# Attention plus recurrence on one core: another order of TensorE's work in the attention slots

## The reference

```python
def attn(x, Wq, Wkv_short, Wkv_long, Wo, mix_weight, decay_factor):   # x: 16 x 512 x 256, 16 heads of 16
    decay_bias = -jnp.abs(pos[None, :] - pos[:, None]) * (1.0 - decay_factor)
    out_short = _attention(q, k_s, v_s, decay_bias)      # softmax(q k^T / 4 + bias) v
    out_long = _attention(q, k_l, v_l, None)
    out = alpha * out_short + (1.0 - alpha) * out_long
    return out @ Wo                                        # heads side by side again
...
x = _layernorm(x + attn(x, ...))
x = _layernorm(x + ffn(x, ...))    # gated recurrence over the 16 sequences, then tanh
```

## Time and profile before

| | |
|---|---|
| median of 3 runs | 2291.74 us (2289.07 to 2291.78) |
| the profiled execution | 2290.99 us |
| its span, first to last instruction | 2289.2 us |
| TensorE busy over the span | 2101.6 us, 92% |
| VectorE busy | 1663.5 us, 73% |
| ScalarE busy | 1476.8 us, 65% |

### The profile page before, as it was taken

One profiled execution on the slowest core, in us unless ns is written; L12 is line 12 of the kernel. 1 busy time (PEld: TensorE's weight loads), 2 busy tenths in 40 slices (PEclk: granted clock), 3 DMA queues, 4 the chain that ended last, 5 costly groups with the idle time before them and its releaser, 6 DMA issues.

```text
span 2289.2 us, 42658 instructions
## 1 busy us (share of the span) xinstructions
PE 2101.6 (92%) x16472; PEld 1126.9 (49%) x16472; DVE 1663.5 (73%) x2106; ACT 1476.8 (65%) x1758; POOL 174.1 (8%) x203
## 2 busy tenths in 40 slices
PE   2999999999999999999999999999999869999950
PEld 1444444444444444444444444444444348888840
DVE  2788888888888888888888788888888723333367
ACT  1477777777777777777777777676767643333336
POOL 0000000000000000000000000000000000000038
PEclk8799999999999999999999999999999979999975
DMA  2222222222222222222222222222222130000017
GB/s 77 47 64 55 53 63 54 62 61 57 63 54 62 54 62 55 62 54 63 55 62 54 62 55 62 64 52 63 53 53 54 36 113 28 27 27 27 18 37 220
DMA packets 127657, 134.27 MB, mean 59 GB/s; under 512 B 39778, under 2 KB 85602, under 8 KB 127474
## 3 DMA queue, kind: packets, MB, share of 16 engines
q1 hardware_dynamic: 98306, 98.74, 18.3%
q10 hardware_dynamic: 29168, 33.03, 4.7%
HBM read 37.77 MB, written 16.78 MB: 24 GB/s over the span
## 4 chain that ended last, share of the span: by engine, by line
PE 86%; ACT 5%; SPq 2%; POOL 2%; issue 2%; DVE 1%; DMA 0%; ACTq 0%; POOLq 0%; DVEq 0%
PE pv_ps L615 22%; PE pair_ps L551 17%; PE work L525 14%; PE pair_ps L577 11%; PE gate_ps L1050 11%; PE work L677 4%; PE pair_ps L533 3%; PE work L1043 2%; ACT probs L327 2%; SPq L199 2%; ACT pv_sb L382 2%; POOL rstd L806 1%; POOL veps L804 1%; PE work L681 1%; PE work L1034 1%
## 5 line engine op out<-in xcount | busy, mean ns | idle before, releaser
L493 DVE TENSOR_REDUCE maxes<-pair_ps 128x2 f32<-128x1024 f32 x1024 | 1247.4, 1223 | 277.4 <-PE pair_ps L533 171.6
L327 ACT ACTIVATE probs<-pair_ps,small 128x1024 f32<-128x1024 f32 x512 | 570.0, 1114 | 250.1 <-PE pair_ps L533 242.8
L327 ACT ACTIVATE probs<-pair_ps 128x1024 f32<-128x1024 f32 x512 | 523.1, 1023 | 180.1 <-PE pair_ps L551 175.8
L615 PE MATMUL pv_ps<-probs,vals 128*32 128x512 f32 x4096 | 547.5, 607 | 0.6 <-ACT probs L327 0.5
L551 PE MATMUL pair_ps<-q_op,k_op 56*128 56x512 f32 (+1 forms) x2048 | 512.4, 498 | 3.6 <-DMA q_op<-shift_rows 2.8
L577 PE MATMUL pair_ps<-k_op,q_op 55*128 55x512 f32 x2048 | 439.4, 425 | 29.3 <-DMA q_op<-kq_l 18.4
L551 PEld LDWEIGHTS pair_ps<-q_op,k_op 56*128 56x128 f32 (+1 forms) x2048 | 191.3, 184 | 554.8 <-issue 525.2
L577 PEld LDWEIGHTS pair_ps<-k_op,q_op 55*128 55x128 f32 x2048 | 196.3, 187 | 94.4 <-ACT probs L327 34.5
L533 PE MATMUL pair_ps<-eye_b,tri_b 64*128 64x64 bf16 x4096 | 152.3, 194 | 0.0
L292 POOL TENSOR_TENSOR o_sum<-o_att 128x512 f32<-128x512 f32 x32 | 40.9, 1278 | 1306.7 <-DVE o_att L460 1306.7
L533 PEld LDWEIGHTS pair_ps<-eye_b,tri_b 64*128 64x128 bf16 x4096 | 90.4, 96 | 92.3 <-issue 72.1
(11 more groups left out here) (129 smaller groups left out, 2467.9 us busy)
## 6 DMA issues: line engine op xcount, KB each, us to landing
k_op<-kq_h SPq DMA_DIRECT2D x1024, 32.0 KB, 2.0
k_op<-kq_l SPq DMA_DIRECT2D x512, 32.0 KB, 2.0
q_op<-kq_h SPq DMA_DIRECT2D x512, 32.0 KB, 2.0
x_step<-in_xT ACTq DMA_DIRECT2D x16, 512.0 KB, 4.1
q_op<-kq_l SPq DMA_DIRECT2D x256, 32.0 KB, 2.0
x_res<-in_x ACTq DMA_DIRECT2D x16, 512.0 KB, 4.6
x_dram<-res ACTq DMA_DIRECT2D x16, 512.0 KB, 3.4
x_back<-x_dram SPq DMA_DIRECT2D x16, 512.0 KB, 4.8
```

The costliest lines, as they stand in the source:

```text
L327: act.activation(probs[:, s % 2, 2 * hp:2 * hp + 2, :], pairs_ps[pair_of(b, s, 2 * hp)][:, :, :], ACT.Exp, scale=LAM if s // 4 % 2 else 1. ...
L493: dve.reduce_max(maxes[:, u % 2, :, hp, s % 4], pairs_ps[pair_of(b, s, 2 * hp + 1)][:, :, :], mybir.AxisListType.X).then_inc(a_reduced, 1)
L615: last = pe.matmul(pv_ps[32 * h:32 * h + 32, :], vals[:, c, g // 2, att, at:at + 32], probs[:, s % 2, h, :], start=(c == 0), stop=(c == TC ...
```

## The change

TensorE's work is written in bodies of two slots. With `s` even, the order is: task of `s`; a stretch of three pairs; `weigh` of slot `s-2`; a stretch of two pairs; `weigh` of slot `s-1`; a stretch of three pairs; task of `s+1`. So the task of an odd slot stands next to the task of the even slot behind it. `weigh` now runs two slots behind (`LAG`), and `probs` has three buffers for two (`PROBS`). In each slot the pair for the maxima now comes ahead of the pair for the weights. The tasks are laid out anew: slots 0 and 28 have none, two slots (23 and 27) do both halves of a `kq`, all `turn` tasks stay at slots 1, 5, ..., 29. On ScalarE the part of the task now comes ahead of both exponentials, and the copy of `pv_ps` moves to slots 1, 5, ..., 29. On VectorE the part of the task stands between the two maxima in odd slots and ahead of both in even slots. The number of matmuls, exponentials and maxima is the same.

```diff
-TASKS = {0: ("ot", 0, -1), 2: ("v", (4,), 0), 3: ("v", (5,), 0), 4: ("v", (6,), 0), 6: ("ot", 1, -1), 7: ("v", (7,), 0),
...
+TASKS = {2: ("v", (4, 5), 0), 3: ("ot", 0, -1), 4: ("v", (6,), 0), 6: ("v", (7,), 0), 7: ("ot", 1, -1), 8: ("wo", (0,), -1),
+         12: ("wo", (1,), -1), 16: ("wo", (2, 3), -1), 20: ("v", (0,), 1), 22: ("v", (1,), 1), 24: ("v", (2,), 1), 26: ("v", (3,), 1),
+         10: ("kq", (1, (0,)), 1), 11: ("kq", (1, (1,)), 1), 14: ("kq", (0, (0,)), 1), 15: ("kq", (0, (1,)), 1),
+         18: ("kq", (2, (0,)), 1), 19: ("kq", (2, (1,)), 1), 23: ("kq", (4, (0, 1)), 1), 27: ("kq", (3, (0, 1)), 1),
+         30: ("kq", (5, (0,)), 1), 31: ("kq", (5, (1,)), 1)}
...
+LAG, PROBS = 2, 3
...
# ScalarE
+                    if s % 4 == 1:
...
+                            act.activation(pv_sb[:, u % 2, :], pv_ps[:, :], ACT.Copy).then_inc(pv_copied, 1)
+                    part_or_values(b, s)
                     if exists(b):
                         exp_pair(b, s, 0)
-                    part_or_values(b, s)
-                    if exists(b):
                         exp_pair(b, s, 1)
...
# VectorE
-                    reduce(0)
+                    if s % 2:
+                        reduce(0)
                     if has_task(b, s):
...
+                    if s % 2 == 0:
+                        reduce(0)
                     reduce(1)
...
# TensorE
             def body(b):
-                for s in range(SLOTS):
-                    scores(b, s, 0)
-                    if has_task(b, s):
-                        work_task(b, s)
-                    scores(b, s, 1)
-                    bb, ss = (b, s - 1) if s else (b - 1, SLOTS - 1)
-                    if exists(bb):
-                        weigh(bb, ss)
+
+                for s in range(0, SLOTS, 2):
+                    work_task(b, s)
+                    scores_for_max(b, s, 0)
+                    scores(b, s, 0)
+                    bias_for_max(b, s, 0)
+                    bias(b, s, 0)
+                    scores_for_max(b, s, 1)
+                    bias_for_max(b, s, 1)
+                    weigh(*weighed(b, s))
+                    scores(b, s, 1)
+                    scores_for_max(b, s + 1, 0)
+                    bias(b, s, 1)
+                    bias_for_max(b, s + 1, 0)
+                    weigh(*weighed(b, s + 1))
+                    scores(b, s + 1, 0)
+                    scores_for_max(b, s + 1, 1)
+                    bias(b, s + 1, 0)
+                    bias_for_max(b, s + 1, 1)
+                    scores(b, s + 1, 1)
+                    bias(b, s + 1, 1)
+                    work_task(b, s + 1)
```

More of the change, by code:

```diff
@@ L102, in pair_of, with held, weighed @@
     return (4 * (b * SLOTS + s) + i) % PAIRS
+def held(b, s, i):
+    for back in (PAIRS, 2 * PAIRS):
+        slot, j = divmod(4 * (b * SLOTS + s) + i - back, 4)
+        bb, ss = divmod(slot, SLOTS)
+        if exists(bb) if j % 2 else exists(unit_of(bb, (ss + AHEAD) // 4)[0]):
+            return j % 2 == 1, bb, ss, j // 2
+    return None
+def weighed(b, s):
+    return (b, s - LAG) if s >= LAG else (b - 1, s - LAG + SLOTS)
 def unit_of(b, u):
@@ L338, in part_or_values @@
                     act.activation(ot_h[:, n, :], work[:, :], ACT.Copy).then_inc(ot_hi, 1)
-                if kind == "kq" and n[1]:
+                if kind == "kq" and 1 in n[1]:
                     m = n[0]
@@ L534, in diagonal, with banks_free, scores @@
                                     eye_b[at:at + HALF, :], start=False, stop=last and half == 1)
-            def scores_of(b, s, hp):
+            def banks_free(b, s, i):
+                last = held(b, s, i)
+                if last:
+                    weights, bb, ss, hp = last
+                    if weights:
+                        wait(pe, exp_done, bb, 2 * SLOTS, 2 * ss + hp + 1)
+                    else:
+                        wait(pe, a_reduced, bb, 2 * SLOTS, 2 * (ss + AHEAD) + hp + 1)
+                return pairs_ps[pair_of(b, s, i)]
+            def scores(b, s, hp):
+                if not exists(b):
+                    return
                 u, c = s // 4, s % 4
                 q, k = q_op[u // 2], k_op[u % RING]
-                banks = pairs_ps[pair_of(b, s, 2 * hp)]
                 if c == 0 and hp == 0:
                     wait(pe, shift_loaded[u % 2], b, 16 * UNITS // 2, 16 * (u // 2 + 1))
-                if exists(unit_of(b, (s + AHEAD) // 4)[0]):
-                    wait(pe, a_reduced, b, 2 * SLOTS, 2 * (s + AHEAD - 1) + hp + 1)
-                else:
-                    wait(pe, a_reduced, B, 2 * SLOTS, 0)
-                    wait(pe, exp_done, b, 2 * SLOTS, 2 * s - 2 + hp)
+                banks = banks_free(b, s, 2 * hp + 1)
                 rows = MAX_ROW + 1 + u % 2
@@ L552, in scores_of @@
                                      start=True, stop=u % 2 == 0)
-                return last, banks
+                if u % 2 == 0:
+                    last.then_inc(b_full, 1)
             def scores_for_max(b, s, hp):
@@ L568, in scores_for_max @@
                         pe.wait_ge(ones_set, 1)
-                if exists(b):
-                    wait(pe, exp_done, b, 2 * SLOTS, 2 * s + hp)
-                else:
-                    wait(pe, a_reduced, b, 2 * SLOTS, 2 * (s + AHEAD) - 2 + hp)
+                banks = banks_free(b, s, 2 * hp)
                 for j in range(2):
@@ L578, in scores_for_max @@
                                      start=True, stop=u % 2 == 0)
-                return last, banks
+                if u % 2 == 0:
+                    last.then_inc(a_full, 1)
             def diagonals(banks, which, c):
@@ L585, in diagonals, with bias, bias_for_max @@
                 return last
-            def scores(b, s, hp):
-                c, short = s % 4, s // 4 % 2
-                here, later = exists(b), exists(unit_of(b, (s + AHEAD) // 4)[0])
-                if here:
-                    b_last, b_banks = scores_of(b, s, hp)
-                    if not short:
-                        b_last.then_inc(b_full, 1)
-                if later:
-                    a_last, a_banks = scores_for_max(b, s, hp)
-                    if not short:
-                        a_last.then_inc(a_full, 1)
-                if short and here:
-                    diagonals(b_banks, 1, c).then_inc(b_full, 1)
-                if short and later:
-                    diagonals(a_banks, 0, c).then_inc(a_full, 1)
+            def bias(b, s, hp):
+                if s // 4 % 2 and exists(b):
+                    diagonals(pairs_ps[pair_of(b, s, 2 * hp + 1)], 1, s % 4).then_inc(b_full, 1)
+            def bias_for_max(b, s, hp):
+                if s // 4 % 2 and exists(unit_of(b, (s + AHEAD) // 4)[0]):
+                    diagonals(pairs_ps[pair_of(b, s, 2 * hp)], 0, s % 4).then_inc(a_full, 1)
             def weigh(b, s):
+                if not exists(b):
+                    return
                 u, c = s // 4, s % 4
@@ L614, in weigh @@
                     at = VW * (GH * (g % 2) + h)
-                    last = pe.matmul(pv_ps[32 * h:32 * h + 32, :], vals[:, c, g // 2, att, at:at + 32], probs[:, s % 2, h, :],
+                    last = pe.matmul(pv_ps[32 * h:32 * h + 32, :], vals[:, c, g // 2, att, at:at + 32], probs[:, (b * SLOTS + s) % PROBS, h, :],
                                      start=(c == 0), stop=(c == TC - 1))
@@ L639, in work_task @@
             def work_task(b, s):
+                if not has_task(b, s):
+                    return
                 kind, n, off = TASKS[s]
```

33 lines of the change are left out of this document (15 added, 18 removed).

## The result

The changed kernel takes 2661.86 us, the median of 4 runs (2651.88 to 2681.4). The kernel before takes 2291.76 us beside it; the ratio is 1.1628, with a 95% interval of 1.1562 to 1.1695. The prediction had the direction, and the time lies inside its range of 2500 to 2710, 72 us above the number given, and above the 2530 to 2650 that it named for the forecast itself. Before, the runs lie within 3 us of each other; now they lie within 30.

What follows compares the result with a forecast made beforehand. TensorE sets the pace: bodies 77.8, junction waits 49.4 and later waits 1.2 make 128.4 us a sequence against 110.9, times 16 giving 280 over 2290.99, so 2571; clock falls add 16, stated as 2590, range 2500 to 2710.

Steps and rivals of the forecast that it cites:

- The bound and the place of the loss: TensorE sets the pace; adjacent tasks wait for the bank `work`; all 16 places together 49.4 us a sequence.
- The three distances: Odd task's start to next even task's: 2.38 us behind half a kq, 1.73 behind a turn, 3.09 behind a double kq.
- some 18: Waits of even slots' first transposes, projections or values for VectorE: some 18 us a sequence together.
- The places without a second task: At slots 28 and 0 the next pair waits for an exponential: Z = X + 2.57, or 3.28 after the double kq.
- 1.2 and 1.2: Waits for maxima a sequence: 0.6 us at both slots 28 and 0; 0.3 and 0.9 after slots 8 and 16.
- The bodies: Two slots without waits, first pair to odd task: long 4.45 us, short 5.28; 77.8 us a sequence.
- The 51 us that the range takes in for the third pair: Upper allowance in the range: a third pair in a stretch costing a first pair's 0.34 us, not 0.24.
- The clock: Each fall costs about 2.5 us; one in five of 32 places (slots 28 and 0) gives 16 us.
- the prediction's own sign: Prediction is wrong if the granted clock is below 1.00 through the middle of the attention.
- the clock gives way in part: Rival: waits are longer or TensorE's clock partly falls, as waits now come every 8 us; chance 0.12.
- The bound of the clock in the range: Allowance for a lower TensorE clock, taken into the upper side of the range 2500 to 2710 us.
- The other side: Rival "fewer changes win": reading out `work` delays nobody, only savings remain, 6.3 us a sequence, 2190 us; chance 0.05.

Runs made afterwards that it cites:

- filler_turn: Changed kernel with zero-adding matmuls on TensorE behind the turns only; 2676.8 us, ratio 1.1678.
- filler: Changed kernel with zero-adding TensorE matmuls behind each odd task, four after a turn, six after a kq or ot; 2577.68 us, ratio 1.1249.
- filler_kq_ot: Changed kernel with zero-adding matmuls on TensorE only behind kq and ot tasks; 2584.89 us, ratio 1.1274.
- max_first: Changed kernel with even tasks moved away from odd ones, and VectorE's first maximum ahead of its part of the odd task; 2298.34 us, ratio 1.0035.
- three_three_two: Changed kernel reordered: three pairs, even task, weigh, three pairs, odd task, two pairs, weigh; weigh one slot behind; 2255.95 us, ratio 0.9845.
- tasks_apart: Changed kernel with each even slot's task moved between the two-pair stretch and the second weigh, so no tasks touch; 2392.07 us, ratio 1.0437.
- half_apart: Changed kernel with the even task moved away only behind a kq or ot (slots 4m), neighbours behind turns kept; 2487.27 us, ratio 1.0856.
- exp_first: Changed kernel with ScalarE making both exponentials ahead of its part of the task in odd slots; 2710.39 us, ratio 1.1861.

## Why the prediction was right, and where it was off

**The bound and the place of the loss: right.** TensorE sets the pace, and two tasks side by side wait for the one bank. The three distances that could be read from single rows come out at 2.38, 1.76 and 3.06 us against 2.38, 1.73 and 3.09. The waits of tasks add up to 190.5 us in 1572 us, 16.3 a sequence, against "some 18"; the counts are eight behind a turn, four behind a `kq`, two behind an `ot` a sequence, as written.

**The places without a second task: right within 0.2 us.** The row of `probs` has two waits a sequence of 1.7 to 1.8 us. Behind slot 31 the pair starts at 1015.57 for a task at 1012.82, so Z = X + 2.75 for 2.57. In filler_turn, whose edit does not touch them, the pair behind the double `kq` starts at 1008.19 for a task at 1004.84, so Z = X + 3.35 for 3.28. Maxima cost 17.7 us in 11.7 sequences, 1.5 each, for the 2.4 of slots 28, 0, 8 and 16 together. That sum had stood as 1.2 and 1.2.

**The bodies: right within 0.07 us.** A short one takes 5.25 us (963.15 to 968.40) for 5.28, a long one 4.52 for 4.45. A third pair costs one step of 0.23 to 0.24 us, with 0.39 (959.47 to 959.86) or 0.33 for the last. The sum by the row was nearer than one with 0.34 for that step. The 51 us that the range takes in for the third pair are that step at 0.34: 0.10 us more for each of two third pairs in 256 bodies. No run shows them; the runs showed 0.23 to 0.24. Two matmuls of full height, each with its own weight load, also start 0.23 us apart in the changed kernel (960.20 to 960.43). At full clock (filler) the whole sequence takes 129.7 us for the 128.4 of the sum, and the kernel 2578 us for 2571.

**The clock: the step that failed.** It stood as "Each fall would cost a low-clock stretch of some 6 us, about 2.5 us of work. One fall in five of these 32 places is 16 us; this is a choice." filler measures that term as 84 us, and the 68 us between the two are nearly all of the 72 by which the number given was too low. By the prediction's own sign (it is wrong "if the granted clock is below 1.00 through the middle of the attention") this part of it was wrong: the windows read 0.95 and 0.96. The chance was the mistake, and the places that were left out. The text took the wait of 0.95 us with the clock at 1.00 for a case like all of its waits and left only slots 28 and 0 as doubtful, at one fall in five. There the clock fell behind 17 waits of 25. And six places a sequence more have waits of 1.4 to 1.5 us, which were put at nothing; 17 of the 34 falls stand behind them. filler_kq_ot and filler_turn show that these eight places carry the cost. The price of one fall was fair for the long stretches alone: 6.9 us at the low clock cost 2.65 us in the one sequence of the changed kernel that holds nothing else (132.35 us against filler's 129.7). In all, 13 sequences hold 38 falls and take 59 us more than 13 of filler, 1.6 us each. The rival "the clock gives way in part" had the mechanism, and a granted clock of 0.95 to 0.96 is its size: 9% of the time at the low level of 0.50. The bound of the clock in the range was the author's estimate and no run shows it; what the runs showed in its place is the 84 us. The sum of the forecast missed the clock, and the width of the range held it; that is in part luck.

**The other side: no, but for a reason that can be priced.** "Fewer changes win" asked for a wait under 0.4 us between two tasks. With the waits gone (max_first) the saving was still not there, since exponentials were late. Part of it came, 2256 us, in an order in which no six pairs stand around one task alone. The 2190 us of that rival were out of reach, by an estimate: a change of kind gave 0.10 us in three_three_two, and it gave no more in the changed kernel: 129.7 us less its 22.0 us of waits (257 us in 11.7 sequences) is 107.7, or 3.2 less than before for two changes fewer in each of 16 bodies. That makes 2240 at best.

**Nothing else was hidden in the change.** The third buffer of `probs` and `weigh` two slots behind are in max_first as well, which ends 7 us from the kernel before.

## What to carry to other kernels

When work that shares one buffer is put side by side, add up the chain that empties the buffer (here 1.0 to 1.4 us of idle time at each place) and look for what covers it; what is saved by fewer changes of kind, 0.1 us each here, is small beside it. After each reordering of the engine that sets the pace, read the orders of the others anew: one and the same order of TensorE (tasks_apart, max_first) was 4.4% slower than before with VectorE's order as it was first written and 0.35% with one maximum moved. And price the clock by how many single waits are long, not by their sum (here a granted clock of 0.94 to 0.95 with some 90 of 1.4 to 1.8 us, 0.99 to 1.00 with 97 of 1.0 us): fill the long ones, or cover them first.

## What the runs showed of the hardware

I had not expected that the same idle time costs so differently. With 97 waits of 1.0 us (filler_kq_ot) TensorE kept a granted clock of 0.99 to 1.00; with some 90 of 1.4 to 1.8 us (filler_turn) it fell to 0.94, and behind such a wait `weigh` took 1.79 us instead of 1.00 (in the changed kernel). The shares of idle time, 9% and 10% by the windows, were nearly the same, and half_apart kept 0.99 with 12%, none of its waits above 1.0 us. The short waits are not quite free: behind them I count two falls in filler_kq_ot and five in half_apart. Nor do longer waits cost more: exp_first, with waits up to 2.8 us, has a clock of 0.94, 0.97 and 0.96 in the three windows, the changed kernel 0.96, 0.95 and 0.96. Work that only adds zero, in the long waits alone, made the kernel 77 us faster (2661.86 to 2584.89). The changed kernel, with one to four falls a sequence, spreads over 30 us from run to run; filler, whose clock never falls in the attention's middle, over 0.8, and filler_turn, where nearly every sequence holds four, over 1.7.
